# A four-layer transformer kernel: the routing steps of runs 0 and 1 moved one slot later in the causal attention, and the first transpose of the expert stage moved ahead of two groups of statistics

## What is computed

```python
x = x + _layernorm(_L0_attn_ref(_layernorm(x), ...))      # causal, 16 heads of 8
x = x + _layernorm(_L0_ffn_ref(_layernorm(x), ...))
# _L0_ffn_ref: one shared expert for every token, 7 routed experts, the best 2 of a token
shared_out = _expert(x, sg, su, sd)                        # silu(x g.T) * (x u.T), then down
logits = x @ wr.T + rb
scores, idx = top_k(softmax(logits), 2); scores = scores / scores.sum()
out = shared_out + sum over e of w[..., e:e+1] * _expert(x, rg[e], ru[e], rd[e])
```

## Time and profile before

| | us |
|---|---|
| three runs | 1046.47, 1043.87, 1046.18 |
| median | 1046.18 |
| the profiled execution, own time | 1044.56 |
| its span, first to last instruction | 1042.80 |
| mean granted TensorE clock, of full speed | 0.962 |

### The profile page before, as it was taken

The page is one execution under the profiler, slowest core; times in us unless marked ns, Lnnn a source line. Parts: engine busy times, 40 slices in busy tenths (PEclk is TensorE's granted clock), DMA queues, the critical chain, the costliest instruction groups (busy, mean ns, idle before and its releaser), DMA issues. The chain is left out here.

```text
span 1042.8 us, 23846 instructions
## 1 busy us (share of the span) xinstructions
PE 929.9 (89%) x8240; PEld 730.2 (70%) x8240; DVE 685.3 (66%) x1910; ACT 518.3 (50%) x1023; POOL 462.1 (44%) x512
## 2 busy tenths in 40 slices
PE   7998989799993899999989999999999977869990
PEld 6666667698993766565776676776766866869990
DVE  4687874565445778888487658676577777764444
ACT  2566654244443378786545545444445434324442
POOL 2355554555445313232463334333456432685443
PEclk9999998999997999999999999999999988989996
DMA  8421100222213024222210011110121820022214
GB/s 276 110 74 56 60 2 2 70 68 68 59 42 87 12 74 140 64 64 66 71 32 2 5 40 43 43 42 3 42 43 42 275 77 1 27 67 72 58 47 121
DMA packets 80750, 66.42 MB, mean 64 GB/s; under 512 B 6706, under 2 KB 73441, under 8 KB 80251
## 3 DMA queue, kind: packets, MB, share of 16 engines
q1 hardware_dynamic: 71899, 54.34, 18.9%
q0 software_dynamic: 4512, 8.47, 2.4%
q10 hardware_dynamic: 4224, 2.10, 0.8%
HBM read 38.76 MB, written 26.58 MB: 63 GB/s over the span
## 5 line engine op out<-in xcount | busy, mean ns | idle before, releaser
L832 DVE TENSOR_REDUCE a_rowmax<-a_banks 128x4 f32<-128x1024 f32 (+1 forms) x112 | 136.8, 1221 | 46.6 <-PE a_banks L1245 19.0
L2897 POOL TENSOR_TENSOR a_both<-a_probs 128x512 f32<-128x512 f32 x64 | 85.7, 1340 | 138.7 <-ACT a_probs L3205 138.6
L1057 ACT ACTIVATE a_probs<-a_banks 128x1024 f32<-128x1024 f32 x112 | 114.8, 1025 | 64.7 <-PE a_banks L1231 48.7
L2182 POOL DMA_INDIRECT acc<-m_result,m_yb x77 | 75.7, 983 | 80.1 <-DVE m_result L2319 40.2
L3205 ACT ACTIVATE a_probs<-a_banks 128x1024 f32<-128x1024 f32 x64 | 65.6, 1025 | 89.7 <-PE a_banks L3376 89.7
L2451 ACT ACTIVATE m_gate<-m_banks 128x352 f32<-128x352 f32 (+1 forms) x93 | 42.8, 460 | 97.8 <-PE m_banks L2612 97.7
L3055 DVE TENSOR_REDUCE a_rowmax<-a_banks 128x4 f32<-128x1024 f32 x64 | 77.8, 1219 | 10.2 <-PE a_banks L3349 10.2
L1712 POOL DMA_INDIRECT rows<-m_yrow,m_idx x64 | 64.8, 1012 | 30.6 <-issue 19.3
L700 POOL TENSOR_SCALAR_AFFINE_SELECT a_probs<-a_probs 128x512 f32<-128x512 f32 (+1 forms) x48 | 37.9, 789 | 76.7 <-ACT a_probs L1057 76.7
L3392 PE MATMUL a_banks<-a_probs,a_V 128*64 128x256 f32 x512 | 69.4, 392 | 0.0
L2304 DVE TENSOR_TENSOR m_h<-m_banks,m_gate 128x342 f32<-128x342 f32 (+1 forms) x55 | 28.5, 517 | 55.5 <-ACT m_gate L2451 43.6
(11 more groups left out here) (420 smaller groups left out, 2552.2 us busy)
## 6 DMA issues: line engine op xcount, KB each, us to landing
rows<-fill SPq DMA_DIRECT2D x16, 520.0 KB, 4.4
a_factor<-recip_rows SPq DMA_DIRECT2D x28, 256.0 KB, 4.7
rows<-fill SPq DMA_DIRECT2D x15, 455.0 KB, 4.2
m_yb<-rows SPq DMA_DIRECT2D x77, 65.0 KB
a_expert<-in_experts SPq DMA_DIRECT2D x16, 257.5 KB, 2.9
e_gu_lo<-in_gu SPq DMA_DIRECT2D x1, 2736.0 KB
e_last_row<-in_last_rows SPq DMA_DIRECT2D x1, 2736.0 KB
e_gu_lo<-in_gu SPq DMA_DIRECT2D x1, 2464.0 KB, 10.2
```

The lines of the kernel that those rows point to most:

```text
L832: nc.vector.reduce_max(o, src, AX).then_inc(rowmax_ready, 1)
L1057: nc.scalar.activation(probs[h][:, k, :, :], ps[:, 4:6, :], ACT.Exp, scale=SCALE).then_inc(exp_done, 1)
L2182: nc.gpsimd.indirect_dma_start(acc.rearrange("k n d -> (k n) d"), bass.IndirectOffsetOnAxis(yb[b % YB][:, P:P + 1].bitcast(U32), 0), resul ...
L2897: nc.gpsimd.tensor_tensor(both[u % 4][:, :, :], p[:, :, 0, :], p[:, :, 1, :], ALU.add).then_inc(both_ready, 1)
```

## The change

1. The routing of run 0 and run 1 in the attention comes later on every engine. TensorE's `turn` of run 0 goes from (9, 1) to (10, 0), its `router` from (9, 3) to (10, 2), its `ranks` from (10, 2) to (11, 0); of run 1 they go from (9, 5), (10, 1) and (10, 4) to (10, 5), (11, 1) and (11, 4). VectorE's and ScalarE's parts move with them. Statistics and norm of both runs stay where they are.
2. The fillers in slots 9 to 12 are other ones. Counting those in `route_step` too, there were 14 in slot 9 (six of them in `route_step`) and 10 in slot 10; there are now 6 and 6. Slots 11 and 12 had 5 each by the table and have 4 each; the six of `step` at (11, 4) and the 16 at the end stay.
3. The two runs use banks 0 and 1 (before: 1 and 0), and a wait of the last row maxima for run 0's logits goes away.
4. In the expert stage the statistics of run 2 come behind the slot event -2, those of run 3 behind the slot event -1; the sends of run 0 and 1 follow piece by piece.

```diff
@@ attention8
-                route.views[r] = Views(ps[:, (1, 0, 1)[r], :], ps[:, (1, 0, 1)[r], :])
+                route.views[r] = Views(ps[:, r, :], ps[:, r, :])
@@ VectorE
             def route_step(s, u):
                 at_step = {(4, 5): ["tables"], (7, 4): ["stats 0"], (8, 3): ["norm 0"], (9, 0): ["stats 1"], (9, 2): ["norm 1"],
-                           (9, 4): ["scores 0"], (9, 5): ["choices 0"], (10, 1): ["share 0"], (10, 2): ["scores 1"],
-                           (10, 3): ["spots 0", "choices 1"], (10, 5): ["share 1", "spots 1"]}
+                           (10, 3): ["scores 0"], (10, 4): ["choices 0"], (11, 1): ["share 0", "spots 0"], (11, 2): ["scores 1"],
+                           (11, 3): ["choices 1"], (12, 0): ["share 1", "spots 1"]}
@@ ScalarE
-                if (s, u) in ((9, 2), (10, 0)):
-                    route.turned(act, ((9, 2), (10, 0)).index((s, u)))
-                if (s, u) in ((10, 0), (10, 4)):
-                    route.ratio(act, ((10, 0), (10, 4)).index((s, u)))
+                if (s, u) in ((10, 1), (11, 0)):
+                    route.turned(act, ((10, 1), (11, 0)).index((s, u)))
+                if (s, u) in ((10, 5), (11, 4)):
+                    route.ratio(act, ((10, 5), (11, 4)).index((s, u)))
@@ TensorE
                 if u == 0 and i2 in valid:
                     pe.wait_ge(stack_ready, 4 * min(ip, SEQS))
-                    if route and i2 == LASTS:
-                        pe.wait_ge(route.logits_read, 1)
                     row_maxima(i2, 1)
...
-            LAST = {SEQS + 1: {0: 2, 1: 3, 2: 3},
-                    SEQS + 2: {0: 2, 1: 2, 2: 2, 3: 2, 4: 2},
-                    SEQS + 3: {1: 3, 3: 2}, SEQS + 4: {0: 3, 2: 2}} if causal else \
+            LAST = {SEQS + 1: {1: 3, 3: 1, 4: 2}, SEQS + 2: {0: 2, 2: 1, 3: 2, 4: 1},
+                    SEQS + 3: {1: 2, 3: 2}, SEQS + 4: {0: 2, 2: 2}} if causal else \
...
-                if (s, u) == (9, 1):
-                    pe.wait_ge(mrow_ready, 2 * (s - 3) + 2)
+                if (s, u) == (10, 0):
+                    pe.wait_ge(mrow_ready, 2 * SEQS - 1)
                     route.turn(pe, 0)
-                if (s, u) == (9, 3):
-                    pe.wait_ge(route.yT_ready, 1)
-                    busy(2, 1)
+                if (s, u) == (10, 2):
                     route.router(pe, 0)
-                if (s, u) == (9, 4):
-                    pe.wait_ge(mrow_ready, 2 * (s - 2) + 1)
-                    busy(2, 0)
-                if (s, u) == (9, 5):
-                    pe.wait_ge(mrow_ready, 2 * (s - 2) + 1)
-                    busy(2, 0)
+                if (s, u) == (10, 5):
+                    pe.wait_ge(mrow_ready, 2 * SEQS)
                     route.turn(pe, 1)
-                if (s, u) == (10, 1):
-                    route.router(pe, 1)
-                if (s, u) == (10, 2):
-                    pe.wait_ge(mrow_ready, 2 * SEQS)
+                if (s, u) == (11, 0):
                     pe.wait_ge(route.logits_read, 1)
                     route.ranks(pe, 0)
-                if (s, u) == (10, 4):
+                if (s, u) == (11, 1):
+                    route.router(pe, 1)
+                if (s, u) == (11, 4):
                     pe.wait_ge(route.logits_read, 2)
                     route.ranks(pe, 1)
@@ shared_first_events
-    events = [("stats", 2), ("stats", 3), ("send", 0), ("send", 1)]
+    behind[-2] = [("stats", 2), ("send", 0, 0)]
+    behind[-1] = [("stats", 3), ("norm", 2), ("send", 0, 1), ("send", 0, 2), ("send", 0, 3), ("send", 1)]
+    events = []
     for n in range(-2, W + 2):
         events += [("slot", n)] + behind.get(n, [])
```

More of the change, by code:

```diff
@@ L1459, in _ @@
                     n = LAST.get(s, {}).get(u, 0)
-                    if causal:
-                        busy(n, {SEQS + 1: 0, SEQS + 2: 2}.get(s, 4))
+                    if causal and n and s == SEQS + 1:
+                        pe.wait_ge(mrow_ready, 2 * (s - 3) + 2)
+                        busy(n, 1)
+                    elif causal:
+                        busy(n, 2 if s == SEQS + 2 else 4)
                     elif n and s == SEQS:
```

## The result

| | before | after |
|---|---|---|
| median of 19 runs each, us | 1043.93 | 1049.41 |
| lowest and highest | 1040.31, 1051.42 | 1044.10, 1060.07 |
| runs above 1050 | 1 | 9 |
| profiled execution, own time | 1044.56 | 1059.43 |
| its span | 1042.80 | 1057.70 |

The ratio after to before is **1.0046, with a 95% interval of 1.0026 to 1.0067**: slower, by 5 us, where 2 us less were forecast, and outside the predicted range.

A forecast was written before the change was run, and what follows sets the result against it. TensorE's queue mostly bounds slot 9, with 10.2 us of low clock and some waits for VectorE. Attention -6.2, expert stage +0.8, low clock +3.4: net -2.0 from 1044.56, 1042.6, plus 1.6 to the median: 1044.2; range 1040.0 to 1048.6.

The forecast's parts named there:

- the idle time ahead of (10, 2): Slot 10: (10, 2) must wait for the exponential of (10, 1), some 1.0 us of TensorE idle time.
- the sum: Attention 6.2 us shorter, expert stage 0.8 later: -5.4 if the clock holds, 4.7 of it from two low stretches.
- share and spots of run 1: Slots 11 and 12, VectorE: these now stand between the last variance and last normalisation, adding 1.0 us.
- +0.8 to the transposes of run 2: Expert stage: these and the first gate matmul come 0.8 us later, as VectorE waits for ScalarE's copy.
- one low stretch as long as the first one: Clock after the change: one low stretch of 6.8 us, costing +3.4; the forecast's case, chance 0.46.
- The price of 0.46: Cost in us of 1 us at the low clock, from two fillers taking 0.85 there and 0.46 at high clock.
- the upper bound of 13.7 us: Most low clock expected, the whole of 161.8 to 175.5 us, twice the observed length, costing 6.4 us.
- the gap of 1.3 us ahead of (9, 2): Slot 9: TensorE idle 0.35 + 1.3 us between (9, 0) and (9, 2), one of the thin places.
- rival 3: Clock falls in slot 9 before (9, 2), low through slot 10: +3.1 or more, 1049.3 us; chance 0.11.
- rival 1: The clock holds through the attention: -5.4, 1040.8 us; chance 0.24.
- Rival 4: Unseen waits take over at (10, 2) and (10, 3), losing 3 us of the gain: 1047 us; chance 0.05.
- three thin stretches: Idle TensorE between (9, 0) and (9, 2), 0.7 to 1.0 us between (10, 1) and (10, 2), 0.7 before (10, 5).

The follow-up runs named there:

- fill10: Changed kernel with two fillers in each of the first five steps of slot 10; 1045.09 us, 0.9994 of before, 3 of 12 runs above 1050.
- waits_filled: Kernel before with 13 fillers at the expert stage's start, three more at (9, 4) and six at (10, 4); 1041.06 us, 0.9952 of before.
- attn_only: Changed kernel with the expert stage's list of events as before; 1051.29 us against 1045.65, ratio 1.0041, 6 of 12 runs above 1050.
- before_thin: Kernel before, routing unmoved, with only the change's number of fillers; 1044.67 us, 0.9999 of before, none of 12 runs above 1050.
- gate_first: Kernel before with the norm of run 2 moved behind slot event 0 in the expert stage; 1045.49 us, 0.9996 of before.
- gap_fill: Changed kernel with five fillers more, all ahead of (9, 2); 1046.03 us, 0.9999 of before, none of 12 runs above 1050.
- narrow_gap: Changed kernel with 11 matmuls of 8 columns added at (9, 0) and (9, 1); 1058.25 us, 1.0116 of before, all 6 runs above 1050.

## Why the prediction was wrong, point by point

**The work at the high clock: right up to slot 10.** fill10 has the changed slot 9 and kept its clock through it, so its rows can be laid beside the forecast, counted from the start of slot 9:

```profile
137.43 0.59 PE L1219 MATMUL a_banks<-a_masks,a_ident 128*128 128x512 bf16 x2 [0.57 <-ACT a_KT L1069]
...
142.67 0.33 PE L1228 MATMUL a_banks<-a_QT,a_KT 25*128 25x128 f32 x2 [1.13 <-DVE a_rowmax L832]
...
149.14 0.39 PE L1231 MATMUL a_banks<-a_QT,a_KT 25*128 25x256 f32 x2 [0.22 <-DVE a_rowmax L832]
...
151.38 0.33 PE L1228 MATMUL a_banks<-a_QT,a_KT 25*128 25x128 f32 x2 [0.72 <-DVE a_rowmax L832]
...
153.94 0.50 PE L1231 MATMUL a_banks<-a_QT,a_KT 25*128 25x256 f32 x4
...
158.31 0.66 PE L1228 MATMUL a_banks<-a_QT,a_KT 25*128 25x128 f32 x8 [0.47 <-ACT a_probs L1057]
```

Its slot 9 starts at 137.43, that of before at 139.08. Step (9, 4) stands 11.7 us behind it (forecast 11.7), (9, 5) 13.95 (14.0), slot 10 16.5 (16.5), (10, 2) 20.9 (20.8). That nothing is gained ahead of (9, 2) also held: 5.2 us in both. No rank matmul waits at (10, 4) any more, but it does at (11, 4), as shown below; the idle time ahead of (10, 2), forecast as about 1 us, is 1.12 in the changed kernel (0.47 here, with two fillers more). The attention without low clock is 42.2 us in the order of before (waits_filled) and, by the prices above, 40.9 to 41.5 with the later routing (fill10): 0.7 to 1.3 shorter, where the sum had 1.5 (6.2 less 4.7 for the clock). Much of what is missing is lost in slot 11, in the next paragraph.

**The end of the attention: mis-sized, and two waits not seen.** The prediction added 1.0 for share and spots of run 1 ahead of the last normalisation. It starts directly behind them, as it said, but 1.26 us behind the start of the variance instead of 0.99: 0.3, since the seven instructions take 1.18 us (197.80 to 198.98) instead of 1.8; the last cast alone takes 0.17 instead of 0.72. Nor does this end the attention: the last residual is done at 200.39 and TensorE's fillers at 200.78. What the prediction left out stands on TensorE ahead of that. First the kernel before:

```profile
181.82 2.03 PE L1195 MATMUL a_banks<-ident 128*128 128x128 f32 x16
...
184.54 0.71 PE L1402 MATMUL a_banks<-w_att,a_cxT 128*128 128x128 f32 x4 [0.47 <-ACT a_cxT L1136]
```

and the changed kernel:

```profile
191.81 2.03 PE L1195 MATMUL a_banks<-ident 128*128 128x128 f32 x16
194.47 0.44 PE L1395 MATMUL a_banks<-ident,a_cx 128*128 128x128 f32 x2 [0.62 <-DVE a_cx L919]
195.33 0.19 PE L1954 MATMUL a_banks<-m_one_hot,m_upper 128*128 128x64 bf16 x1 [0.43 <-DVE m_chosen L1812]
...
195.62 0.69 PE L1400 MATMUL a_banks<-w_att,a_cxT 128*128 128x128 f32 x4
```

The last transposes of the attention wait for VectorE's `a_cx`, which now stands behind the scores of run 1, and the ranks of run 1 wait for `m_chosen` again, 0.43 us ahead of the last output matmuls. From these fillers to TensorE's first instruction of the expert stage it is 10.00 us instead of 9.15, at the high clock in both: 0.85 longer. The prediction counted the ranks (0.3) there, but neither wait.

**The expert stage: right.** Forecast +0.8 to the transposes of run 2, measured 6.24 instead of 5.57, +0.7, for the reason given: `low_y` of block 0 waits for ScalarE's copy, and everything on VectorE behind it. Not foreseen: 6.8 us of low clock at that start instead of 3.4. It does not come from the new order, since attn_only, before_thin and gate_first have the old one and 6.8 too. Part of the +0.7 goes with it: in attn_only and before_thin the transposes of run 2 come after 5.82 and 5.81 us, which leaves 0.4 for the order alone.

**The clock: this is the step that failed.** "I take one low stretch as long as the first one, 6.8 us, since it is the nearest row in place and mixture: +3.4". In the profiled execution it was 44.4 us; at the measured 0.38 each that is 17 us in place of 3.4. The 34 more than before cost 13, less what the work gained, and the attention is 11.8 longer. (The price of 0.46, from two fillers, is a little high for this mixture.) Two things were wrong in it. The place: the forecast put the fall in slot 10, and the upper bound of 13.7 us was worked out for that alone. The text named the gap of 1.3 us ahead of (9, 2) (it is 1.13) and made it rival 3, with 0.11, "Against: the rest of slot 9 is dense". It is not dense in the sense that matters: gap_fill shows that the rest of slot 9 keeps a clock that is high, the changed kernel that it does not bring back one that is low. And the length: the 6.8 us came from a row of before, where fillers and transposes stood behind the fall, and those were part of what had gone. Rival 3 had 20 us, "from 145 to 165", "through slot 10"; but by the prediction's own starts slot 10 ends near 171 even at the high clock, and at the low clock its work took longer still, to 187.8.

**The starting point.** The forecast of 1044.2 started from the median of three runs, 1046.18; over 19 runs the kernel before has 1043.93. So the time was missed by 5 us, and the change by more: 2.0 faster forecast, 5 slower measured.

**Falls and gaps.** Before, the clock fell behind a longest gap of 0.74 us; with the change behind 1.13 us, and in narrow_gap with TensorE busy for 5.00 of the 5.00 us ahead of it. The Trainium skill, TensorE: Matmul & The Clock Gate, section "Why this matters for your kernels", warns of long idle gaps between bursts. By that alone the clock would have held, with the time of rival 1, 1040.8; the traces disagree.

**The rivals and the chances.** Rival 3 happened in the profiled run, in mechanism and place, though with twice its length of low clock. That the median of 1049.4 lies on its 1049.3 is accident: the runs spread from 1044 to 1060, 9 of 19 above 1050, and a single time was the wrong picture. (Where the runs without a profile lost their time is not seen; that emptying this gap moved all of them to 1056 and filling it all to 1046 is what ties the spread to it.) Rival 4 (unseen waits) did not come at (10, 2) and (10, 3), its places, but two such waits came in slot 11, 1.05 us together. The net that the new order gives at the high clock, 0.7 to 1.3 in the attention less 0.7 in the expert stage, is at most 0.6 us (the prediction had 0.7): too little to carry that risk. The prediction lists the gap ahead of (9, 2) first among its three thin stretches, and then works out a time and bounds for the second alone; the 0.11 of rival 3 was too low for a place that the change had thinned by two fillers and four transposes.

**What stays open.** Why the same kernel keeps its clock at (9, 2) in one run and not in the next is not shown; no run here varies it by itself. Whether denser work in slot 10 makes the long runs rarer (3 of 12 against 15 of 31) is open too. And the kernel before has long runs itself, 19 of 121 beside the experiments; no profile of it caught one, so where they lose their time is not seen.

## What to carry to other kernels

Where an engine's queue holds fillers, take a moved instruction for what it also is, a filler at its old place: count what is left between two points of waiting, not the fillers over a slot. Price a clock fall by what stands behind it in the new order, and if the work there is narrow, expect it to last (44.4 us here, where the rows of before gave 6.8). And read the scatter of many runs, not only the median: a kernel near this edge shows it as a wide spread of times, 1044 to 1060 here. If a change gains a few tenths of a microsecond and thins such a place, put the filler back: the five in gap_fill's wait cost nothing, since (9, 2) stands 5.2 us behind the start of slot 9 with and without them.

## What the runs showed of the hardware that was not expected

- A low clock can last while TensorE is nearly always busy: 42.68 of 44.00 us in the changed kernel, with products of 32 rows, transposed scores of 25 rows, picks of 36 columns. It came back at 187.8, at the end of slot 10, behind the transposes of run 1; in attn_only, with the same instructions, it came back at 165.3 too, for 3.4 us. What it takes to bring it back is not shown.
- Narrow matmuls do not stand in for fillers: 11 of 8 columns added in the gap left all 6 runs above 1054, five fillers of 128 columns added in it left none of 12 above 1048.
- A step of this kind is steep: three fillers taken from (9, 1) moved all runs to 1055 to 1058, two added at (9, 0) moved all but one of 12 below 1050.
- Thirteen fillers in two waits of the expert stage's start, 3.2 us of matmuls that are not read, made the kernel before faster, 0.9956 (0.9926 to 0.9987), at a place that the change had not aimed at. waits_filled, with nine more in the attention, has 0.9952, which can't be told from it.
